# First attention of a fused four-layer kernel: raw turned rows, centred query weights, 256-column scores, and turned keys and probabilities placed behind the next key projection

## The reference

```python
def _L0_xattn_ref(text, features, Wq_w, Wq_b, Wk_w, Wk_b, fn_w, qn_w, kn_w):
    features_n = rmsnorm(features, fn_w)
    Q = jnp.einsum('btd,fd->btf', text, Wq_w) + Wq_b
    K = jnp.einsum('bsd,fd->bsf', features_n, Wk_w) + Wk_b
    Q = rmsnorm(Q, qn_w)
    K = rmsnorm(K, kn_w)
    scores = jnp.einsum('btf,bsf->bts', Q, K) * scale
    attn = jax.nn.softmax(scores, axis=-1)
    return jnp.einsum('bts,bsf->btf', attn, features_n)

x = x + _L0_xattn_ref(_layernorm(x, axis=-1), ctx_4096, ...)   # this layer
x = x + _L0_ffn_ref(_layernorm(x, axis=-1), ...)               # sparse feed-forward
x = x + _L1_xattn_ref(...)                                     # 32-head attention
x = x + _L1_ffn_ref(...)                                       # clustered feed-forward
```

## Time and profile before

| | us |
|---|---|
| median of three runs | 1509.6 (1509.44 to 1510.46) |
| the profiled execution: its own time | 1511.27 |
| its span | 1509.5 |
| of this, up to the first matmul of step 1 | 36.9 |
| steps 1 to 14 of the first attention | 133.6 |
| from the end of step 14 to the end | 1339.0 |

### The profile page before, as it was taken

One profiled execution on the slowest core, in us unless ns is written; L12 is line 12 of the kernel. 1 busy time (PEld: TensorE's weight loads), 2 busy tenths in 40 slices (PEclk: granted clock), 3 DMA queues, 4 the chain that ended last, 5 costly groups with the idle time before them and its releaser, 6 DMA issues.

```text
span 1509.5 us, 27579 instructions
## 1 busy us (share of the span) xinstructions
PE 1463.2 (97%) x9895; PEld 846.4 (56%) x9895; DVE 1127.8 (75%) x2172; ACT 795.1 (53%) x3201; POOL 710.3 (47%) x668
## 2 busy tenths in 40 slices
PE   5999999999999799999999999999999999999998
PEld 4888745555555455555555555555565555555554
DVE  5788787878876888776776676677677677667868
ACT  5678841211223576556546654754664565565763
POOL 5668875454565353334334343433434333343553
PEclk9999999999999999999999999999999999999999
DMA  7454435333344565653553554455445445334622
GB/s 248 147 175 136 123 81 126 98 77 50 65 88 72 117 147 84 110 119 64 100 105 53 95 88 81 86 87 95 81 80 105 79 73 103 64 60 67 99 50 112
DMA packets 358936, 146.87 MB, mean 97 GB/s; under 512 B 342304, under 2 KB 342688, under 8 KB 356112
## 3 DMA queue, kind: packets, MB, share of 16 engines
q1 hardware_dynamic: 357504, 137.77, 45.1%
q10 hardware_dynamic: 1296, 7.34, 1.5%
HBM read 58.02 MB, written 4.19 MB: 41 GB/s over the span
## 4 chain that ended last, share of the span: by engine, by line
PE 55%; DVE 5%; ACT 3%; DMA 1%; POOL 1%; issue 1%; SPq 0%; DVEq 0%; POOLq 0%; ACTq 0%
PE bank L72 18%; PE bank L74 17%; PE bank L73 17%; PE bank L2439 3%; ACT a_prob L1836 2%; DMA a_pT_lo<-a_p_lo 1%; POOL a_prob L1707 1%; DVE a_oT_lo L2106 1%; DVE x_res L2193 1%; DVE a_qve L2045 1%; ACT a_oT_lo L1813 0%; DVE a_p_lo L2094 0%; DVE a_nmx L2082 0%; DVE a_qr_lo L2035 0%; POOL a_xr_lo L1731 0%
## 5 line engine op out<-in xcount | busy, mean ns | idle before, releaser
L1836 ACT ACTIVATE a_prob<-a_prob,a_nmx 128x64 f32<-128x64 f32 x512 | 170.2, 334 | 183.7 <-DVE a_nmx L2082 183.7
L72 PE MATMUL bank<-w,a_oT_hi 128*128 128x512 f16 x512 | 194.0, 379 | 1.8 <-DVE a_oT_lo L2106 0.9
L74 PE MATMUL bank<-w,a_oT_hi 128*128 128x512 f16 x512 | 194.0, 379 | 0.0
L73 PE MATMUL bank<-w,a_oT_lo 128*128 128x512 f16 x512 | 194.0, 379 | 0.0
L72 PE MATMUL bank<-w,xT_hi 128*128 128x448 f16 (+1 forms) x512 | 188.0, 367 | 3.1 <-DVE h L1231 2.0
L73 PE MATMUL bank<-w,xT_lo 128*128 128x448 f16 (+1 forms) x512 | 187.7, 367 | 0.0
L74 PE MATMUL bank<-w,xT_hi 128*128 128x448 f16 (+1 forms) x512 | 187.5, 366 | 0.0
L1707 POOL TENSOR_TENSOR a_prob<-a_prob,a_mask 128x512 f32<-128x512 f32 x64 | 79.8, 1268 | 204.5 <-DVE a_prob L2076 204.5
L2031 DVE SCALAR_TENSOR_TENSOR x_res<-bank,a_oinv,x_res 128x512 f32<-128x512 f32 x128 | 95.5, 746 | 75.0 <-PE bank L74 75.0
L1157 ACT CAST f_h_hi<-h 128x448 f16<-128x448 f32 x64 | 35.6, 563 | 209.7 <-DVE h L1231 209.6
L1719 POOL TENSOR_TENSOR a_krs<-a_kve,neg_half 128x4 f32<-128x4 f32 x32 | 32.8, 1026 | 239.6 <-DVE a_kve L2056 239.6
(11 more groups left out here) (351 smaller groups left out, 4120.5 us busy)
## 6 DMA issues: line engine op xcount, KB each, us to landing
shared<-in_l_wq SPq DMA_DIRECT2D x8, 1024.0 KB, 5.0
shared<-in_l_wo SPq DMA_DIRECT2D x8, 1024.0 KB, 5.1
shared<-in_w ACTq DMA_DIRECT2D x8, 896.0 KB, 4.7
craw<-in_w SPq DMA_DIRECT2D x11, 512.0 KB, 3.9
a_wide<-in_l_ctxT SPq DMA_DIRECT2D x16, 256.0 KB, 4.0
x_res<-in_x SPq DMA_DIRECT2D x16, 256.0 KB, 4.5
shared<-in_ctx SPq DMA_DIRECT2D x16, 256.0 KB, 4.4
shared<-in_l_wkv SPq DMA_DIRECT2D x8, 512.0 KB, 3.9
```

Source lines behind the costliest of these rows:

```text
L72: pe.matmul(out, a_hi, b_hi, start=first, stop=False)
L73: pe.matmul(out, a_lo, b_hi, start=False, stop=False)
L74: return pe.matmul(out, a_hi, b_lo, start=False, stop=last)
L1836: ins = act.activation(pt, pt, ACT.Exp, bias=nmx[:, col:col + 1], accum_out=den[:, col:col + 1])
```

## The change

- The rows are no longer normalised ahead of the query projection. The host gives the raw `x` turned (`l0_xT`), SP loads it (16 loads of 256 KB), ACT casts it (line 517) and POOL (tiles 0 to 7, line 427) or DVE (tiles 8 to 15, line 656) subtracts. `normalise`, PE's turn of the rows and POOL's shift are gone.
- The mean is taken out of the weights instead: POOL adds the blocks of the raw query weights (414), DVE adds the two sums (824), a PE matmul with a matrix of 1/512 makes the mean of each column (one matmul of 512 columns on float32 operands), DVE subtracts it from each block (815), and only then are the weights split. The root of the variance is applied in `query_bias` (671).
- Scores take 8 matmuls of 256 columns, qT_hi and qT_lo each against kT_hi and kT_lo side by side; DVE adds the two halves with one more instruction (731).
- `k_T(n)` and the turn of tile n-1's probabilities stand behind `project_k(n+1)`; DVE's and ACT's orders follow.
- POOL takes `features_lo(n)` and `weigh(n+1)` at the head of step n, and no longer waits there for `scale_keys`.
- In the last full step, tile 14's, `attend(13)` comes after `q_T(15)`, `k_T(15)` and the turn of the next layer's rows.

The core of the diff:

```diff
@@ scores and order on PE
         def body(n, first=False, ahead=True, project=True):
             if project and not first:
+                pe.wait_ge(s_kb, n + 1)
                 project_k(n + 1)
+            if n != NT - 1:
+                k_T(n)
+            if not first:
+                probs_T(n - 1)
+            if project:
                 project_q(n + 1)
             pe.wait_ge(s_kTl, n + 1)
             if not first:
                 pe.wait_ge(s_pTl, n)
             for k in range(KD):
-                ins = split_mm(pe, b_s[:, 0:P], qT_hi[:, k, :], qT_lo[:, k, :], kT_hi[:, k, :], kT_lo[:, k, :],
-                               k == 0, k == KD - 1)
+                pe.matmul(b_both, qT_hi[:, k, :], kT_both[:, k, :], start=k == 0, stop=False)
+                ins = pe.matmul(b_both, qT_lo[:, k, :], kT_both[:, k, :], start=False, stop=k == KD - 1)
             ins.then_inc(s_s, 1)
-            if ahead:
-                rows_T(n + 2)
-            if not first:
+            if not first and n != NT - 2:
                 attend(n - 1)
             if project:
                 q_T(n + 1)
+            if n == NT - 2:
                 k_T(n + 1)
+            if n in PREP_AT:
+                first_rows_T(PREP_AT[n])
+            if n == NT - 2:
+                attend(n - 1)
...
         project_k(0, first=True)
-        rows_T(0)
-        project_q(0, first=True)
+        pe.wait_ge(s_mean, 3)
+        pe.matmul(w_mean[:, :], thin[:, :], w_sum, start=True, stop=True).then_inc(s_mean, 1)
         pe.wait_ge(s_kb, 1)
         project_k(1)
+        project_q(0, first=True)
         q_T(0)
@@ POOL
         def body(n, first=False, ahead=True, project=True):
+            features_lo(n)
+            if project:
+                weigh(n + 1)
             tile_roots(n)
             if ahead:
                 features_T(n + 2)
             if project:
                 key_root(n + 1)
-                pool.wait_ge(s_kn, n + 2)
...
-            if project:
-                features_lo(n + 1)
-            if ahead:
-                weigh(n + 2)
+            if ahead and n + 2 < POOL_ROWS:
+                rows_T(n + 2)
@@ DVE
         def rows_T(n):
             dve.wait_ge(s_xTh, n + 1)
-            dve.tensor_tensor(xT_lo[:, :, :], blk(bxT), xT_hi[:, :, :], ALU.subtract).then_inc(s_xTl, 1)
+            dve.scalar_tensor_tensor(xT_lo[:, :, :], xT_raw[n % 2][:, :, :], 1.0, xT_hi[:, :, :], ALU.mult, ALU.subtract)\
+                .then_inc(s_xTl, 1)
...
             dve.scalar_tensor_tensor(prob[:, :], b_s[:, 0:P], qrs(n), off[:, :], ALU.mult, ALU.add).then_inc(s_nmx, 1)
-            dve.wait_ge(s_nmx, n * 2 + 1)
+            dve.wait_ge(s_nmx, n * 3 + 1)
+            dve.scalar_tensor_tensor(prob[:, :], b_s[:, P:2 * P], qrs(n), prob[:, :], ALU.mult, ALU.add).then_inc(s_nmx, 1)
+            dve.wait_ge(s_nmx, n * 3 + 2)
             dve.tensor_reduce(nmx[:, :], prob[:, :], AX.X, ALU.max, negate=True).then_inc(s_nmx, 1)
...
+        def centre_wq(k):
+            dve.tensor_tensor(w_raw[0][:, k, :], w_raw[0][:, k, :], w_mean[:, :], ALU.subtract).then_inc(s_mean, 1)
```

More of the change, by code:

```diff
@@ L446, in pool_steps @@
         features_T(0)
-        first_row_root(0)
+        add_wq(w_sum, 0)
+        add_wq(w_high, 1)
         first_features_root(0)
         features_T(1)
+        rows_T(0)
         key_root(0)
+        first_row_root(0)
+        weigh(0)
         first_features_root(1)
+        rows_T(1)
         first_row_root(1)
-        weigh(0)
-        first_row_root(2)
-        features_lo(0)
-        weigh(1)
         pool.wait_ge(s_eps, 1)
@@ L486, in squares_c @@
             act.activation(sq, craw[:, bass.ts(n % 2, D)], ACT.Square, scale=MEAN, accum_out=css(n)).then_inc(s_css, 1)
-        def normalise(n):
-            if n < 3:
-                act.wait_ge(s_first_sh, n + 1)
-            else:
-                act.wait_ge(s_root, n - 2)
-            if n:
-                act.wait_ge(s_xT, n)
-            act.activation(xn[:, :], m.x[:, bass.ts(n, D)], ACT.Identity, bias=sh(n), scale=rs(n)).then_inc(s_xn, 1)
         def features(n):
@@ L663, in attended @@
             xt = m.x[:, bass.ts(n, D)]
-            dve.scalar_tensor_tensor(xt, b_att[:, :], rden[:, :], xt, ALU.mult, ALU.add).then_inc(s_x, 1)
+            dve.scalar_tensor_tensor(xt, b_att[:, :], rden[:, n % 2:n % 2 + 1], xt, ALU.mult, ALU.add).then_inc(s_x, 1)
         def body(n, first=False, ahead=True, project=True):
-            if project:
-                key_bias(n + 1)
-            if n + 4 < NT:
-                statistics(n + 4)
+            if n >= 2:
+                attended(n - 2)
+            if not first:
+                denominator(n - 1)
+            q_T(n)
+            if n == 6:
+                w1_scales()
+            if n == NT - 2:
+                w2_scales()
+            if project and not first:
+                key_bias(n + 1)
+            k_T(n)
+            if n - 1 in PREP_AT and n == NT - 1:
+                first_rows_T(PREP_AT[n - 1])
+            if not first:
+                probs_T(n - 1)
+            if n + 3 < NT:
+                statistics(n + 3)
             if project:
                 query_bias(n + 1)
-            if n == NT - 2:
-                scale_keys(n + 1)
             dve.wait_ge(s_s, n + 1)
@@ L795, in dve_steps @@
         query_bias(0)
-        qk_T(0)
-        rows_T(1)
+        key_bias(1)
+        statistics(1)
         statistics(2)
-        statistics(3)
         run(body)(dve)
+        attended(NT - 2)
+        denominator(NT - 1)
+        probs_T(NT - 1)
         before_last()
@@ L804, in pe_steps @@
     def pe_steps(pe, filler):
-        def rows_T(n):
-            pe.wait_ge(s_xn, n + 1)
-            for k in range(KD):
-                ins = pe.transpose(bxT[:, k * P:(k + 1) * P], xn[:, k * P:(k + 1) * P], m.ident[:, :])
-            ins.then_inc(s_xT, 1)
         def project_k(n, first=False):
```

311 lines of the change are left out of this document (167 added, 144 removed).

## The result

| | kernel before | changed kernel |
|---|---|---|
| median | 1509.1 us (1506.1 to 1513.2, 20 runs) | 1512.1 us (1508.9 to 1513.4, 20 runs) |
| profiled execution | 1511.3 us | 1513.2 us |
| its span | 1509.5 us | 1511.0 us |
| mean granted clock | 0.994 | 0.991 |

The ratio is 1.0019, with a 95% interval of 1.0013 to 1.0025: 3 us slower, where 11 us faster was forecast, and outside the range. From the turn of the last tile's probabilities on, the two traces take equally long (1511.0 - 177.08 = 1333.9 us against 1509.5 - 175.67 = 1333.8), so all that differs inside the span happened in the first 177 us. A further 0.4 us lies outside the span: an execution is 1.8 us longer than its span before and 2.2 us now (1513.19 - 1511.0), the latter in all 20 executions within 0.05 us.

What follows compares the result with a forecast made beforehand. PE was taken to bound the steps, with DVE close behind. Start -4.4, steps 1 to 5 -5.5, steps 6 to 13 -4.0, step 14 0.0, end +3.0: -10.9 us, median 1498.7, range 1488 to 1510.

Steps and rivals of the forecast that it cites:

- Steps 1 to 5: First five tile steps, PE-bound at 8.22 us plus 0.24 each: 42.3 us against 47.84, a gain of 5.5.
- the meeting of `scale_keys` and `features_lo`: DVE and POOL instructions due together in a step; charged 0.24 us a step in steps 1 to 5.
- Steps 6 to 13: DVE 8.4 us a step plus 0.7 for two meetings with POOL: 72.8 us against 76.82, -4.0.
- Step 1's clock: Step 1 at full clock thanks to shorter PE gaps: 2.4 us of the 5.5 gained in steps 1 to 5.
- The start: Loads, sums and weight splits up to step 1's first matmul: 32.5 us against 36.9, -4.4.
- The chain through the mean: At the start: POOL's sums done about 14.0 us, DVE's 0.7, float32 matmul 1.5, subtractions and splits 5.2.
- Step 14 and the end: Step 14 at 8.9 us against 8.94, counted 0.0; the reordered last steps cost +3.0 (1 to 4).
- The distance between the last two scores: On PE, from tile 14's scores to tile 15's: 6.9 us against 3.7 before, +3.2.
- Outside the span: Execution time not in the profiled span: 1.8 us, left alone by the change.
- Rival 2: DVE and POOL block each other fully each time: -1.4 us, 1508.2; steps 6 to 13 at 9.7; chance 0.18.
- Rival 3: Both DVE SBUF pairs wait behind whole POOL instructions: steps 6 to 13 at 10.6, +9.8 us, 1519.4; chance 0.08.
- Rival 4: A 256-column score matmul costs like a 512-column one, 0.227 us: steps of at least 9.08, 1506.8; chance 0.04.

Runs made afterwards that it cites:

- experiment 3: Changed kernel plus six unread 512-column matmuls on PE ahead of the score wait in steps 5, 9, 11 and 13: 1512.1 us, ratio 1.0015.
- experiment 6: Changed kernel with scale_keys reading its weights from PSUM (except tile 15) and attend(13) back ahead of q_T(15): 1500.2 us, ratio 0.9931.
- experiment 10: experiment 6 with ACT's scaling of two weight pieces (steps 11 and 13) moved back behind query_squares: 1496.7 us, ratio 0.9912.
- experiment 2: Changed kernel with POOL's old wait put back, features_lo waiting until DVE has scaled the next tile's keys: 1505.6 us, ratio 0.9972.
- experiment 4: Changed kernel with attend(13) back in its usual place, ahead of q_T(15): 1510.0 us, ratio 1.0004.
- experiment 9: Changed kernel with ACT's scaling of two weight pieces (steps 11 and 13) moved back behind query_squares: 1509.8 us, ratio 0.9997.
- experiment 11: Kernel before with one line gone, POOL's wait for the scaled keys ahead of features_lo: 1519.4 us, ratio 1.0064.
- experiment 1: Changed kernel with scale_keys reading its weights from a PSUM copy, so one SBUF input instead of two, except tile 15: 1503.8 us, ratio 0.9960.
- experiment 12: experiment 10 plus unread matmuls on PE in its last two waits, ahead of k_T(15) and tile 15's scores: 1498.7 us, ratio 0.9910.

## Why the prediction was wrong, point by point

**Steps 1 to 5: 42.3 forecast, 47.4 measured.** This is the step that failed first: the price of the meeting of `scale_keys` and `features_lo`. PE's own work was right: the 256-column matmuls are 0.12 apart, and a full step takes 8.15 to 8.17. The hold was also seen, but charged at 0.24 us a step, "most of it within DVE's slack". There was hardly any slack, 8.1 us of DVE in a step of 8.22, and the meeting happens nearly every step, at 1.0 us when DVE comes just second. Steps 2 to 4 took 9.07, 8.92 and 8.87, which is 8.1 and most of one full hold. Step 5 is 3.9 of the 5.1 us: it took 12.37 where 8.46 was forecast, with DVE late from the steps before, its extra work on the maxima of the next layer's weights (whose copy, L762, was held too, 1.15 us instead of 0.29), and PE at the lower clock; at the full clock it took 10.8 (experiment 3). Experiment 6, without the hold, takes 41.6 for all five and 8.94 for step 5.

**Steps 6 to 13: 72.8 forecast, 81.85 measured.** I took the middle between no hold and two, 0.7 us; DVE lost 0.64 us in each `scale_keys` and 0.96 in each rows' subtraction, 1.6 a step. Experiment 6 gives 6.2 us of the 9.1 back and removes only the first of them: the subtraction then falls to 1.15 by itself. Another 3.8 us came back with ACT's waits for its weight pieces (75.64 to 71.86, experiment 10); step 11 had also been at the lower clock in experiment 6, which is in these 3.8. Those I had not looked for: I had counted the scaling as moved and not set its new place beside the time at which its load lands.

**Step 1's clock.** I counted on 2.4 us from the full clock, and got it. That the clock fell again in other steps was not foreseen; experiment 3 puts its cost at nothing by the medians and at 2.3 us by the traces.

**The start: first matmul of step 1 at 32.5 forecast, 30.45 measured.** The chain through the mean was cheaper at each link: POOL began the sums at 8.74 and was done by 11.7, not at 14.0, and the float32 matmul began at 12.48 and was recorded with 1.17 us, where I took 1.5.

```profile
8.74 2.93 POOL L414 TENSOR_TENSOR a_wide<-x_res 128x512 f32<-128x512 f32 x2 [3.27 <-DMA x_res<-in_l_wq]
```
```profile
12.48 1.17 PE L948 MATMUL bank<-a_wide,a_prob 128*128 128x512 f32 x2
```

Profiles of kernels with the same start have this matmul of step 1 between 30.4 and 32.3 (experiments 2, 3, 4 and 9), so part of the 2 us is scatter.

**Step 14 and the end: 0.0 and +3.0 forecast, +3.4 measured for the two.** From the first matmul of tile 15's key projection to the turn of its probabilities PE took 177.08 - 159.64 = 17.44 us, against 175.67 - 161.59 = 14.08. The distance between the last two scores was forecast at 6.9 and is 7.06; of that the order is worth 1.8. This part of the working held.

**Outside the span: nothing forecast, +0.4 measured.** I took the 1.8 us before as a constant; it is 2.2 in the changed kernel, and no run shows why.

**Rival 2,** full blocks, had the right mechanism and 0.18 of the chance. Its own sum, 1508.2, was still 4 us short, with steps 6 to 13 at 9.7 where they took 10.2; ACT's wait was in no case. **Rival 3,** both of DVE's pairs held by whole instructions, gave 10.6 us for steps 6 to 13, where 10.2 was measured. Against it I had argued that an idle POOL frees DVE; but in experiment 11 one root releases both, and they met in 11 of 14 steps. In the changed kernel the root ends earlier (46.51 in step 2, against 47.73 and 47.80 for the two starts), and yet eight of 14 `scale_keys` took over 1.6 us; what keeps the two in step there no run shows. The two together deserved more than 0.26. **Rival 4** is out: 0.12, not 0.227.

The sum of the misses: 5.1 and 9.0 in the steps and 0.4 at the end, against 2.1 at the start, is 12.4 us inside the span, and 0.4 outside it. The median is 13.4 us above the forecast; the 0.6 that is left is within the scatter of single executions.

## What to carry to other kernels

A wait that looks like waste may be what keeps two engines off a shared resource: before counting a removed wait as a gain, list which instructions run beside each other without it, and charge the full overlap when one engine's release starts both. Where DVE is within a few tenths of the bound, as here, such a hold lands in the time; moving one input of the instruction to PSUM was worth 8 us here and costs one bank. And when work is reordered on an engine, set each moved instruction beside the landing time of what it reads, not only beside its own length.

## What the runs showed of the hardware

- A DVE instruction of 128 x 512 float32 with two SBUF inputs that starts while POOL runs ends 0.54 to 0.55 us behind POOL's instruction (three meetings above, behind POOL instructions of 1.26, 1.30 and 1.91 us); with one of its inputs in PSUM it takes 0.74 beside the same POOL work (experiment 1). POOL's instruction, when it is second, is held too (1.69 against 1.29).
- A copy on DVE with its input and output in SBUF (128 x 256 float32) took 1.15 us in the changed kernel, where it began 0.28 us after POOL's split of the context and ended 0.15 behind it, and 0.29 in the kernel before and in experiment 1. An instruction of two columns with one SBUF input (L769) took 1.25 beside POOL in experiment 3 and 0.17 in the changed kernel.
- A float32r matmul of 256 columns takes 0.12 us at the full clock, where 128 columns take 0.108 and 512 take 0.227: the narrow one is charged nearly as much as the double.
- The granted clock fell behind a wait of 1.83 us in the changed kernel and stayed at 1.00 behind one of 1.82 in the same place in experiment 4. In two of four pairs of steps the fall cost nothing, in the other two 0.75 and 1.53 us by the traces; in a last step on PE's own path it cost 1.6 us (6.65 against 5.09, experiment 12).
